# The product of the first two layers and the label product in rounded high and low halves, W2 by blocks, the table chain early

## What is computed

```
x = x + conv(x; log_dt, C, log_A_real, A_imag, D)          # state space layer, masked by length
x = x + x @ W1.T + 2 * sum_e gate_e * (x @ A_lang[e].T) @ B_lang[e].T
x = x + x @ W2.T + 0.5 * (x @ A_lab[label]) @ B_lab.T
x = x + x @ w_eff.T        # w_eff: W3 + lora, quantized to a codebook of 64 values with group scales, + lora
```

## Time and profile before

| | |
|---|---|
| median of 3 runs | 1021.84 us (1021.79 to 1021.91) |
| profiled execution | 1022.23 us, its span 1020.4 us |
| PE busy | 997.8 us (98%) |
| DVE busy | 819.7 us (80%) |
| ACT busy | 460.2 us (45%) |
| POOL busy | 282.5 us (28%) |
| granted TensorE clock, mean | 0.998 |

### The profile page before, as it was taken

How to read it: one execution, slowest core, us unless ns; L and a number is a source line. 1 busy time by engine, 2 the same in 40 slices (tenths; PEclk the granted TensorE clock), 3 DMA queues, 4 the chain that set the end, 5 groups by cost and what they waited for, 6 DMA issues and landing times.

```text
span 1020.4 us, 16368 instructions
## 1 busy us (share of the span) xinstructions
PE 997.8 (98%) x4767; PEld 797.0 (78%) x4767; DVE 819.7 (80%) x1617; ACT 460.2 (45%) x867; POOL 282.5 (28%) x343
## 2 busy tenths in 40 slices
PE   6999999999999999999999999999999999999997
PEld 3455558888888778888888888888888888888875
DVE  5499898989865788888888888888788888888861
ACT  1452524452366454445453454435544354443531
POOL 6300100644444322332223222232222322233100
PEclk9999999999999999999999999999999999999999
DMA  8602010100203344544445444454545545455311
GB/s 294 119 22 82 1 42 1 42 1 5 38 3 59 62 87 79 102 87 81 84 83 103 82 84 80 91 100 77 89 76 102 93 73 92 75 104 90 60 33 42
DMA packets 314516, 74.44 MB, mean 73 GB/s; under 512 B 290402, under 2 KB 307106, under 8 KB 314482
## 3 DMA queue, kind: packets, MB, share of 16 engines
q1 hardware_dynamic: 313554, 73.42, 36.6%
q10 hardware_dynamic: 928, 0.62, 0.3%
HBM read 57.08 MB, written 16.91 MB: 73 GB/s over the span
## 4 chain that ended last, share of the span: by engine, by line
PE 94%; ACT 2%; DVE 2%; issue 1%; ACTq 1%; DMA 0%; SPq 0%; DVEq 0%
PE bank L713 34%; PE bank L918 13%; PE bank L860 11%; PE bank L703 10%; PE bank L734 4%; PE bank L683 4%; PE bank L672 4%; PE bank L694 3%; PE bank L740 2%; PE bank L871 2%; PE bank L840 2%; PE bank L724 1%; PE bank L800 1%; PE bank L879 1%; PE bank L661 1%
## 5 line engine op out<-in xcount | busy, mean ns | idle before, releaser
L713 PE MATMUL bank<-Mh,strips_r 128*128 128x512 f32 x1024 | 289.8, 395 | 0.0
L713 PEld LDWEIGHTS bank<-Mh,strips_r 128*128 128x128 f32 x1024 | 190.7, 188 | 41.3
L991 ACT ACTIVATE SK<-ZZ 64x448 f32<-64x448 f32 x128 | 73.9, 577 | 212.7 <-DVE ZZ L1321 210.3
L495 POOL TENSOR_TENSOR Cl<-QC,Ch 128x256 fp32r<-128x256 f32 x32 | 37.2, 1163 | 453.8 <-ACT Ch L973 453.8
L713 PE MATMUL bank<-Ml,strips_r 128*128 128x512 f32 x512 | 160.6, 395 | 0.0
L1321 DVE SCALAR_TENSOR_TENSOR ZZ<-ZZ,coef 128x192 f32<-128x192 f32 (+1 forms) x256 | 121.2, 513 | 10.1 <-DVE ZZ L1312 0.3
L713 PEld LDWEIGHTS bank<-Ml,strips_r 128*128 128x128 f32 x512 | 96.2, 188 | 22.7
L860 PE MATMUL bank<-E,A 128*128 128x512 f32 (+1 forms) x352 | 112.1, 477 | 0.8 <-ACT A L1060 0.8
L703 PE MATMUL bank<-Mh,strips_r 128*128 128x296 f32 x512 | 110.4, 299 | 0.2 <-DVE strips_r L1340 0.2
L860 PEld LDWEIGHTS bank<-E,A 128*128 128x128 f32 x352 | 56.8, 191 | 51.6 <-issue 50.2
L703 PEld LDWEIGHTS bank<-Mh,strips_r 128*128 128x128 f32 x512 | 85.0, 189 | 5.4 <-issue 5.2
(11 more groups left out here) (295 smaller groups left out, 1800.2 us busy)
## 6 DMA issues: line engine op xcount, KB each, us to landing
X<-in_x SPq DMA_DIRECT2D x256, 64.0 KB, 2.6
XT<-in_x SPq DMA_DIRECT2D x256, 64.0 KB, 2.5
out_x<-O SPq DMA_DIRECT2D x64, 256.0 KB, 3.2
toep<-kpad SPq DMA_DIRECT2D x128, 64.0 KB, 2.1
E<-in_L_cond_W SPq DMA_DIRECT2D x8, 512.0 KB, 9.1
vq<-in_L_cond_weight SPq DMA_DIRECT2D x8, 512.0 KB, 3.4
W2s<-in_L_cond_W SPq DMA_DIRECT2D x7, 512.0 KB, 4.4
LA<-in_L_cond_lora_A SPq DMA_DIRECT2D x8, 80.0 KB, 3.6
```

The source lines that it names most:

```text
L713: pe.matmul(psO[nh][:, :], xs[:, c, :], ms[:, c, nh * BANK:(nh + 1) * BANK], start=(c == 0 and n == 0), stop=False)
L991: act.activation(SK[ri * N:(ri + 1) * N, hh, :].rearrange("p (c b) -> p c b", b=B), ZZ[hh * N:(hh + 1) * N, :, ri, :], ACT.Copy).then_inc( ...
```

## The change

1. **Halves.** `E1`, `A2` and the label matrix `LA` are each kept as a rounded high half (`E1h`, `A2h`, `LAh`, float32r) and a low half, the value minus the high half. ScalarE rounds, GpSimd subtracts. Each product is three float32r products: high by high, and the two mixed ones.
2. **W2 by blocks.** `A2` is no longer whole: three places of one 128-column block each, with a full copy `A2raw` for the subtraction. ScalarE copies each staged half twice. The identity is now added to `W2s` before the transposes.
3. **The table chain.** The small exponentials and angles leave GpSimd for VectorE, before it takes `codes`; what was `nat_rest()` now stands ahead of quarter 0. `nat_sine()` follows `("w2t", 1, 1)`.
4. **Order.** `at`, `wrt` and all deltas from quarter 1 on come later; `deltas(2)` and `deltas(3)` lie between `lap` 4 to 8. `over` has three places; over[1] lies on `dq[0]`, over[2] and over[3] on quarter 0. Comparisons and `init_quarter` move accordingly. SyncE issues W2's block 3 before `A_nat`, `Wr_nat` and `BwIn`.

```diff
-        order += [("at", 0), ("at", 1), ("wrt",)]
-        between = {2: deltas(1)[:2], 3: deltas(1)[2:], 5: [("nat4",)] + deltas(2)[:2], 6: deltas(2)[2:]}
+        between = {2: [("at", 0), ("at", 1), ("wrt",)], 3: deltas(1)[:2], 4: deltas(1)[2:], 5: [("nat4",)]}
...
-        order += deltas(3)[:2]
         for mt in range(MT):
-            order += [("lap", mt)] + ([("a3", 0, mt)] if mt < 4 else [])
-        order += deltas(3)[2:]
+            order += [("lap", mt)]
+            order += [("a3", 0, mt)] if mt < 4 else [] if mt == MT - 1 else (deltas(2) + deltas(3))[2 * mt - 8:2 * mt - 6]
...
+                def e1_low(it):
+                    pool.wait_ge(e1_hi, it + 1)
+                    pool.tensor_tensor(E1l[:, it, 0:L], E1raw[:, it, 0:L], E1h[:, it, 0:L].bitcast(F32), ALU.subtract).then_inc(e1_lo, 1)
...
+                def a2_low(ot):
+                    n = a2_place(ot)
+                    for half in range(2):
+                        its = slice(4 * half, 4 * half + 4)
+                        pool.wait_ge(stage_free, jobno[("w2t", ot, half)] + 1)
+                        pool.tensor_tensor(A2l[n][:, its, :], A2raw[n][:, its, :], A2h[n][:, its, :].bitcast(F32), ALU.subtract).then_inc(a2_lo, 1)
...
+                w2_diagonal(0)
                 e1_diagonal(0)
...
+                a2_low(0)
+                for it in range(1, NC):
+                    e1_diagonal(it)
+                    e1_low(it - 1)
+                e1_low(NC - 1)
+                for ot in (1, 2):
+                    w2_diagonal(ot)
+                    a2_low(ot)
...
+                        for n in range(2):
+                            pe.matmul(bank[2 + n][:, :], A2h[0][:, it, :], E1h[:, it, n * BANK:(n + 1) * BANK], start=(it == 0), stop=False)
+                        for n in range(2):
+                            pe.matmul(bank[2 + n][:, :], A2l[0][:, it, :], E1h[:, it, n * BANK:(n + 1) * BANK], start=False, stop=False)
+                        pe.wait_ge(e1_lo, it + 1)
+                        for n in range(2):
+                            last = pe.matmul(bank[2 + n][:, :], A2h[0][:, it, :], E1l[:, it, n * BANK:(n + 1) * BANK], start=False, stop=(it == NC - 1))
...
-                        last = pe.matmul(bank[2 + 3 * (kt % 2) + n][:, 0:b - a], A2[:, it, kt * P:(kt + 1) * P], E1[:, it, a:b],
-                                         start=(it == 0), stop=(it == NC - 1))
+                        for m, (w, e) in enumerate(((A2h, E1h), (A2h, E1l), (A2l, E1h))):
+                            last = pe.matmul(bank[2 + 3 * (kt % 2) + n][:, 0:b - a], w[k][:, it, :], e[:, it, a:b],
+                                             start=(it == 0 and m == 0), stop=(it == NC - 1 and m == 2))
...
-                        if n == 0 and q >= 2:
-
-                            act.wait_ge(quant_done, q - 1)
+                        if n == 0 and q == 2:
+
+                            act.wait_ge(v_used, QT_TILES + 1)
+                        elif n == 0 and q == 3:
+
+                            act.wait_ge(quant_done, 2)
...
+                        act.activation(A2h[a2_place(ot)][:, its, :], stage(j)[:, :].rearrange(rows, t=4), ACT.Copy)
+                        act.activation(A2raw[a2_place(ot)][:, its, :], stage(j)[:, :].rearrange(rows, t=4), ACT.Copy).then_inc(stage_free, 1)
+                        if j == ("w2t", 1, 1):
+                            nat_sine()
+                        elif j == ("w2t", 3, 1):
+                            compare(0, 0)
+                            compare(0, 1)
+                        elif j == ("w2t", 7, 1):
                             compare(1, 2)
                             compare(1, 3)
...
+                        if name == "qt0":
+                            for it in range(which[0] * NC // 2, (which[0] + 1) * NC // 2):
+                                act.wait_ge(e1_diag, it + 1)
+                                act.activation(E1h[:, it, 0:L], E1raw[:, it, 0:L], ACT.Copy).then_inc(e1_hi, 1)
...
+                        if kt == 0:
+                            init_quarter(0)
...
-                        if q == 0 and 4 <= mt < 4 + FIXED:
-                            compare(3, mt - 4)
+                        if q == 0 and 1 <= mt < 1 + FIXED:
+                            compare(2, mt - 1)
+                        elif q == 1 and 2 <= mt < 2 + FIXED:
+                            compare(3, mt - 2)
...
-                    if q == 0:
-                        nat_rest()
```

More of the change, by code:

```diff
@@ L140, in resid_stack_kernel, with a2_place @@
     assert cursor[0] <= after_lowrank
+    at_quant = [region_q + 4 * ((3 + q) * QCOLS + 2 * 1024) for q in range(QUARTERS)]
     over = [nc.alloc_sbuf_tensor_at(f"above{n}", [P, FIXED, QCOLS], U8, offset=at)
[L144 to L147, removed]
+            for n, at in enumerate((at_quant[1], region_q + 4 * QCOLS, at_quant[0]))]
+    over.append(over[2])
+    scale8 = place("scale8", [NC, P * NC], F32, at=at_quant[1])
+    B3n = place("B3n", [P, NC, R3], F32)
+    A3raw = place("A3raw", [R3, L], F32, at=region_carry + 4 * EW)
+    W2s = place("W2s", [P, 2, L], F32, at=at_quant[3])
+    A2h, A2raw, A2l = [], [], []
+    for n, at in enumerate((region_q + 8 * QCOLS, region_q - 4 * NC * QO, at_quant[2])):
+        A2h.append(place(f"A2h{n}", [P, NC, P], F32R, at=at))
+        A2raw.append(place(f"A2raw{n}", [P, NC, P], F32))
+        A2l.append(place(f"A2l{n}", [P, NC, P], F32R, at=at + 4 * NC * P))
+    def a2_place(kt):
+        return 0 if kt == 0 else 1 if kt % 2 else 2
     HH = H // 2
@@ L533, in a2_diagonal @@
[L533 to L543, removed]
@@ L584, in _ @@
[L584 to L591 removed]
+                    d = E1raw[:, it, it * P:(it + 1) * P]
@@ L869, in lap, with one @@
                     if mt == 0:
-                        pe.wait_ge(ld_la, 16 * NC)
-                    several(("lap", mt), NC, lambda ps, it: pe.matmul(
-                        ps[:, 0:LR], E1[:, it, mt * P:(mt + 1) * P], LA[:, it, :, :].rearrange("p l r -> p (l r)"),
-                        start=(it == 0), stop=(it == NC - 1)))
+                        pe.wait_ge(la_lo, 1)
+                    def one(ps, n):
+                        it, m = n // 3, n % 3
+                        w, a = ((E1h, LAh), (E1h, LAl), (E1l, LAh))[m]
+                        return pe.matmul(ps[:, 0:LR], w[:, it, mt * P:(mt + 1) * P], a[:, it, :], start=(n == 0), stop=(n == 3 * NC - 1))
+                    several(("lap", mt), 3 * NC, one)
                 def a3(q, n):
@@ new lines, in _ @@
+                step(dve.scalar_tensor_tensor(nat4[:, 3, lo_n], t0, 2.0, t2, ALU.mult, ALU.mult))
+                step(dve.scalar_tensor_tensor(nat4[:, 2, hi_n], t0, 2.0, t2, ALU.mult, ALU.mult))
+                for s in range(2):
+                    cols = slice(s * N, (s + 1) * N)
+                    step(dve.tensor_copy(nat4[:, 0, cols], dtA_re))
+                    last = dve.tensor_copy(nat4[:, 1, cols], dtA_im)
+                    if s == 0:
+                        step(last)
+                last.then_inc(nat4_ready, 1)
```

239 lines of the change are left out of this document (99 added, 140 removed).

## The result

The changed kernel takes **1066.38 us** (median of 4 executions, 1063.71 to 1069.74) against 1021.88 for the kernel before: ratio 1.0434 [1.0409, 1.0459], 44.5 us slower. The forecast was 1049 with a range up to 1066: the direction and most of the mechanism were right, the size was 14 to 17 us short.

The account below looks back on a forecast made before the run. TensorE was taken to bound the kernel before, with GpSimd pacing the changed start. Delays through quarter 2's deltas, VectorE's quarters and the tables (28.8 late, 1.5 slack) summed to 27 us more: 1022.23 + 27 = 1049.2, so 1049, range 1031 to 1066.

Parts of the forecast that it names:

- the language half: TensorE stops 2.2 us for the low half of the language columns, made on GpSimd.
- TensorE from 44.1 to the last delta of quarter 2: TensorE's work and stops from the start of qt(1, 0) put quarter 2's last delta at 186.5, usable by VectorE at 187.5.
- Sum 129.5. Stops: ...: Ahead of quarter 2, TensorE's jobs take 129.5 us; stops of 2.2, 3.9 and 6.8 add 12.9.
- What would show it: Signs: qt0 ends near 37, qt(1, 0) starts near 44, clock at upper level, VectorE gap about 18, TensorE stop about 10.
- TensorE is delayed by almost as much behind `state_transpose(0)`: Behind quarter 3, tab_pow comes 28.8 us late and TensorE is delayed nearly as much, with 1.5 allowed for slack.
- narrow products by columns: Rival, chance 0.12: 128-column float32r products take 0.07 us each instead of 0.107, giving 1037 us.
- no slowing: Rival, chance 0.10: VectorE and GpSimd do not slow each other in the quarters and tables, giving 1033 us.
- Slow GpSimd: Rival, chance 0.12: GpSimd's 128 x 1024 subtraction takes 3.75 us, making qt0 12.5 later and the time 1065 us.
- TensorE's work alone decides: Rival, chance 0.08: TensorE's saving of 11.3 us in work reaches the end, giving a faster 1010.5 us.

Follow-up runs that it names:

- e9_again: The changed kernel measured once more with nothing edited: 1063.3 us, ratio 1.0402 to the kernel before.
- e3_busy_waits: Changed kernel with float32r products nobody reads added in five of TensorE's waits: 1059.0 us, ratio 1.0360 to the kernel before.
- e1_deltas_early: Changed kernel with quarter 2's deltas right ahead of the label product, quarter 3's behind laps 4 and 5, quarter 2's comparisons behind laps 4 to 7: 1058.9 us.
- e10_deltas_refilled: Changed kernel with quarter 2's deltas ahead of the label product, quarter 3's behind laps 6 and 7, comparisons respread, unread products in waits except ahead of a3(3, 0): 1048.5 us.
- e2_compare_early: Changed kernel with comparisons 2 and 3 of quarter 0 taken behind the copies of QT's block 2: 1064.1 us, ratio 1.0395 to the kernel before.
- e7_chain_late: Changed kernel with VectorE's table chain, nat_sin to nat4, put behind quarter 0 again: 1060.3 us, ratio 1.0364 to the kernel before.
- e12_best: Changed kernel with first product block in float32, quarter 0's deltas later, quarter 2's and 3's deltas and the comparisons of quarters 0, 2 and 3 moved: 1041.4 us.
- e4_halves_split: Changed kernel with each of GpSimd's eight 128 x 1024 subtractions in the first product made as two of 128 x 512: 1062.4 us, ratio 1.0411 to the kernel before.

## Why the prediction was short

**Right.** GpSimd paces the start: 128 x 1024 took 2.36 (2.35 forecast), two of 128 x 512 2.49 (2.5), the identity 0.45. `nat_sine` and the B3 halves come before the first deltas, `wrt` waits for the comparisons (3.1 and 3.6, forecast 3.9), the language half costs a stop of 2.23 (2.2). VectorE waits for quarter 2's deltas (19.3, forecast 18), TensorE for quarter 3 (9.3, forecast 10). The narrow products do not shrink with their columns: starts 0.11 apart (0.107 forecast), and so are those of 160 columns. The 81 ns of the Trainium skill ("TensorE: Matmul & The Clock Gate", section "Back-to-back issue gap") are not met here; 0.111 is. Rows of the changed kernel:

```profile
99.74 0.27 PE L852 MATMUL bank<-E1h,A2l 128*128 128x128 f32 x1
99.85 0.27 PE L852 MATMUL bank<-E1h,A2h 128*128 128x128 f32 x1
```

Quarters 2 and 3 took 106.2 together (forecast 106.5).

**The step that failed** is "TensorE from 44.1 to the last delta of quarter 2", with its "Sum 129.5. Stops: ..." and the line of "What would show it" that puts TensorE's clock "at its upper level as now". It priced every stop at its length and every product at the upper clock. The stops brought the clock to its lower level, and the products behind them took twice as long: 5.49 instead of 2.76 for `qt(1, 0)`, 10.50 instead of 5.3 for the 48 narrow ones, 16.13 instead of 13.64 for the 72 behind `wrt`. That is 2.7 + 5.2 + 2.5 = 10.4 ahead of quarter 2 in the first profile, and 2.7 + 0.3 + 1.8 = 4.8 in e9_again; behind `a3(3, 0)` 1 to 3 more. e3_busy_waits shows the cause, e1_deltas_early and e10_deltas_refilled the price of small stops (7 for two of 1.6, 3 for one).

**A second step failed**, behind quarter 3: "TensorE is delayed by almost as much behind `state_transpose(0)`". It led the delay through the tables. They took 34.9 (forecast 38), which gained nothing, since nothing waited for them: they end at 343.8, and ScalarE begins the first tile's columns 4.4 later, as soon as it has copied the `m` product that stands before them in its list and for which it waited for TensorE. Rows of ScalarE in the changed kernel:

```profile
347.61 0.38 ACT L1228 ACTIVATE Mh<-bank 128x256 fp32r<-128x256 f32 x1 [2.79 <-PE bank L914]
...
348.15 0.42 ACT L1074 ACTIVATE X1T<-rem 64x256 f32<-64x256 f32 x1
```

So TensorE's own jobs from `a3(3, 0)` on set `low_in`. They took 70.0 before and 76.3 here (74.8 in e9_again). The clock was at 0.88 for the first 11 us, and TensorE stopped once more, for nothing that the profile names (a piece of the chain):

```profile
332.92 2.37 issue
```

The forecast has 73.4 from the end of quarter 3 to `low_in` (367.4 less 294), the profile 76.4, 3.0 more.

**Terms that were mis-sized.** `qt(1, 0)` at 46.2 instead of 44.1: the small operations of VectorE were charged as if alone, and GpSimd held them for 1.2 to 2.3 us each, so the places came at 25.8 instead of about 15.7 and made the turn through `codesT` and ScalarE a stop of GpSimd of 3.5 instead of 2.1; TensorE then waited 2.1 at `codes` for `sel`, which the prediction does not have. The prediction charged sharing from quarter 0 on only. The label jobs 2.86 instead of 24 x 0.107 = 2.57, 1.7 in six. The narrow products 0.111 instead of 0.107, 0.8 in 192. Quarter 0's start was 65.9 instead of 58.5 and its wait 14.2 instead of 5.6 (7.1 in e9_again): 14 us later than forecast at the start of quarter 1, and worth nothing, as e2_compare_early and e7_chain_late show.

With 187.5 as forecast for quarter 2, 2.1 + 10.4 + 1.7 + 0.8 make 202.5, measured 202.6; in e9_again 2.4 + 4.8 + 1.7 + 0.8 make 197.2, measured 196.9. So close a fit is partly luck. Counted from start to start in the first profile, TensorE has 82.7 us of wide products (78.1 charged), 26.3 of narrow ones (20.5), 16.4 of label jobs (15.4; 0.7 of the 1.7 above falls to the jobs behind them in this count), 20.3 of transposes, deltas and other small jobs (15.5) and 9.3 of idle time (12.9), 155.0 instead of 142.4. The small jobs came out 4.8 above their price and the stops 3.6 below, and the short sum leaves out both. With the 3.0 behind quarter 3, the 15.1 ahead of quarter 2 make up the 17.9 by which `low_in` was later than forecast, but for 0.2.

**The rivals.** Neither the narrow products by columns nor no slowing came true. "Slow GpSimd", 1065, gave nearly the time but by a mechanism that was not there: in the first product its subtractions ran at the forecast price. Later pairs of 128 x 512, beside VectorE's passes, took up to 7.3 instead of 2.5, but TensorE did not wait for them. "TensorE's work alone decides" is refuted for this kernel; in e10_deltas_refilled and e12_best, where TensorE waits for almost nobody from 70 us on, it does decide, and the time is still 27 and 20 us over that of before.

**What stays open.** Why the same stop leaves the clock at 0.50 for 11 us in one execution and at 0.96 in another of the same program was not found; the profile shows the level, not its reason. It was also not tried to keep float32 for the narrow and the label products alone, since the rounded low halves lie where the unrounded operands lay.

## What to carry to other kernels

Price a stop of TensorE as its length plus what the clock may take behind it: here one wait of 1.65 us cost 3 more, two of 1.64 cost 7 more, the removal of one of 3.6 gained about 4 in all, and the sum differs from execution to execution. When a faster form of an operation needs helpers (here rounding on ScalarE, low halves on GpSimd), cost the helpers' queue first: 2.36 us of GpSimd a block against 1.4 of TensorE decided the start, and further stops (at `wrt`, between the laps) came from ScalarE having one more thing to do between two takes. And when two chains hand over to each other, look for where one already waits for the other before moving work: 14 us won in quarter 0 came back as waits of 9.5 and 6.6 in quarter 1, and the 7 us of the table chain vanished in the wait ahead of quarter 2.

## What was not expected of the hardware

The executions of one program differ by up to 8 us, and their mean granted clock with them (1059.3 to 1067.1 in e4_halves_split, at 0.983 and 0.975), where the kernel before, without stops, stays within 2.9 in 11 executions (clocks of 0.995 to 0.999). At the lower level both the wide products (0.43 apart) and the narrow ones (0.21 apart) take about twice as long as at the upper (0.23 and 0.11), so the floor of the narrow ones, too, follows TensorE's clock. And a VectorE operation on 64 columns with one operand, 0.20 us alone, took 2.30 beside a GpSimd subtraction and 1.19 beside one of half the length.
